# A perceiver block on one core: small sums leave TensorE for GpSimd, ScalarE and VectorE

## The reference

```python
def xattn(encoder_hc, decoder_hq, w_sim, b_sim, W_qv, b_qv):   # encoder_hc = layernorm(x), decoder_hq = ctx
    w1, w2, w3 = w_sim[:d], w_sim[d:2*d], w_sim[2*d:]
    Sim = (encoder_hc @ w1)[:, :, None] + (decoder_hq @ w2)[:, None, :] \
        + einsum('bid,bjd->bij', encoder_hc * w3, decoder_hq) + b_sim[0]
    A = softmax(Sim, axis=2)
    hq_hat = einsum('bij,bjd->bid', A, decoder_hq)
    Batt = softmax(max(Sim, axis=2), axis=1)
    hc_bar = einsum('bi,bid->bd', Batt, encoder_hc)[:, None, :]
    feats = concatenate([encoder_hc, hq_hat, encoder_hc * hq_hat, encoder_hc * hc_bar], axis=-1)
    return feats @ W_qv + b_qv
x = x + xattn(layernorm(x), ctx, ...)
x = x + linear_attention_with_rope(layernorm(x), ...)   # 16 heads
x = x + channel_mix(layernorm(x), ...)                  # token shift, relu squared, sigmoid gate
```

## Time and profile before

| | |
|---|---|
| median of 3 runs | 112.9 us (112.89 to 113.84) |
| the profiled execution's own time | 112.94 us |
| its span in the profile | 111.2 us |
| first pass, second pass, tail | to about 45 us, to about 91 us, to the end |

### The profile page before, as it was taken

The page is one execution under the profiler, slowest core; times in us unless marked ns, Lnnn a source line. Parts: engine busy times, 40 slices in busy tenths (PEclk is TensorE's granted clock), DMA queues, the critical chain, the costliest instruction groups (busy, mean ns, idle before and its releaser), DMA issues.

```text
span 111.2 us, 1842 instructions
## 1 busy us (share of the span) xinstructions
PE 105.4 (95%) x580; PEld 85.2 (77%) x581; DVE 93.6 (84%) x153; ACT 81.3 (73%) x170; POOL 26.2 (24%) x44
## 2 busy tenths in 40 slices
PE   5899999999999999999999999999999998998890
PEld 2368777676757668888989999898989997887680
DVE  1488999989999999989999999999999846684342
ACT  5076755889979986999999899989986625903450
POOL 2239100000023334124242423367230000100100
PEclk9999999999999999999999999999999999999999
DMA  3999999999999999999999999950000000000001
GB/s 79 382 410 422 420 416 423 420 420 420 410 422 417 420 413 420 422 404 398 439 401 410 422 422 420 414 201 3 3 0 0 0 6 0 0 0 3 6 0 47
DMA packets 8220, 29.82 MB, mean 268 GB/s; under 512 B 1042, under 2 KB 1298, under 8 KB 8082
## 3 DMA queue, kind: packets, MB, share of 16 engines
q1 hardware_dynamic: 8064, 29.69, 66.0%
q10 hardware_dynamic: 146, 0.01, 0.1%
HBM read 29.57 MB, written 0.13 MB: 267 GB/s over the span
## 4 chain that ended last, share of the span: by engine, by line
PE 91%; DVE 2%; DMA 2%; issue 1%; ACT 1%; POOL 1%; DVEq 0%; POOLq 0%; ACTq 0%
PE mixed_ps L988 18%; PE scores_ps L959 10%; PE mixed_ps L990 9%; PE scores_ps L916 9%; PE scores_ps L945 8%; PE scores_ps L931 8%; PE scores_ps L935 8%; PE scores_ps L970 3%; DMA x_sb<-x_dram 2%; PE scores_ps L1081 2%; PE mixed_ps L1133 2%; PE side_ps L1007 1%; PE scores_ps L1146 1%; PE side_ps L1124 1%; PE scores_ps L1007 1%
## 5 line engine op out<-in xcount | busy, mean ns | idle before, releaser
L689 DVE TENSOR_TENSOR pair<-raw,pair 128x1024 fp32r<-128x1024 f32 (+1 forms) x41 | 49.4, 1220 | 1.4 <-ACT pair L486 1.4
L486 ACT ACTIVATE pair<-raw 128x512 fp32r<-128x512 f32 (+1 forms) x41 | 33.3, 814 | 6.6 <-DMA raw<-keys_dram 5.1
L988 PE MATMUL mixed_ps<-pair,turned_high 128*128 128x512 f32 x84 | 32.3, 418 | 0.0
L990 PE MATMUL mixed_ps<-pair,turned_low 128*128 128x256 f32 x84 | 23.6, 281 | 0.0
L461 POOL CAST pair<-raw 128x512 fp32r<-128x512 f32 x22 | 13.6, 618 | 27.2 <-DVE pair L689 23.9
L988 PEld LDWEIGHTS mixed_ps<-pair,turned_high 128*128 128x128 f32 x84 | 15.8, 188 | 2.8
L712 DVE TENSOR_SCALAR_CACHE_REDUCE neg_scores<-scores_ps,neg_max 128x1024 f32<-128x1024 f32 (+2 forms) x14 | 16.0, 1145 | 0.4
L518 ACT ACTIVATE turned_high<-scores_ps 128x512 fp32r<-128x512 f32 (+1 forms) x23 | 13.4, 584 | 3.9 <-PE scores_ps L959 3.9
L990 PEld LDWEIGHTS mixed_ps<-pair,turned_low 128*128 128x128 f32 x84 | 16.0, 190 | 0.0
L719 DVE TENSOR_TENSOR turned_low<-scores_ps,turned_high 128x512 fp32r<-128x512 f32 (+1 forms) x23 | 15.3, 669 | 0.2 <-ACT turned_high L518 0.2
L959 PE MATMUL scores_ps<-ident,neg_scores 128*128 128x128 f32 x98 | 14.6, 272 | 0.0
(11 more groups left out here) (189 smaller groups left out, 129.6 us busy)
## 6 DMA issues: line engine op xcount, KB each, us to landing
raw<-keys_dram SPq DMA_DIRECT2D x24, 512.0 KB, 10.6
raw<-rows_dram SPq DMA_DIRECT2D x24, 512.0 KB, 8.7
w<-weights_dram SPq DMA_DIRECT2D x1, 1792.0 KB, 9.5
w<-weights_dram SPq DMA_DIRECT2D x2, 512.0 KB, 11.5
const<-const_dram SPq DMA_DIRECT2D x1, 832.0 KB, 10.9
raw<-keys_last_dram SPq DMA_DIRECT2D x1, 256.0 KB, 9.5
raw<-rows_last_dram SPq DMA_DIRECT2D x1, 256.0 KB, 6.1
x_sb<-x_dram SPq DMA_DIRECT2D x1, 128.0 KB, 2.3
```

The source lines that it names most:

```text
L486: nc.scalar.activation(pair[:, use % PAIR_BUFS, 0, 0:columns], raw[:, slot(item), 0:columns], ACT.Copy)\
L689: nc.vector.tensor_tensor(out=pair[:, use % PAIR_BUFS, 1, 0:columns], in0=raw[:, slot(item), 0:columns], in1=pair[:, use % PAIR_BUFS, 0, 0 ...
L988: nc.tensor.matmul(mixed_ps[:, :].rearrange("p (h d) -> p h d", h=2), probs_high, both[:, :, t * D:(t + 1) * D], start=(k == EARLY and t = ...
L990: last = nc.tensor.matmul(mixed_ps[:, 0:D], probs_low, rows_tile(high, t), start=False, stop=(k == LATE - 1 and end))
```

## The change

Three parts.

1. **hw1.** The three matmuls and the little load of b_sim go. A load of 128 equal rows of w1 and b_sim (128 x 257) is issued by SP behind keys 13. GpSimd multiplies `normed` by it ahead of its part of chunk 18, as soon as VectorE has chunk 15's low part; ScalarE sums the product behind chunk 19's high part; VectorE adds b_sim in the instruction that makes `sim_max`.
2. **Token attention.** ScalarE takes the exponential of all 128 spread columns in PSUM, with their sum. TensorE's three matmuls of round 8 go. In round 10 VectorE makes two fused products with a sum (`normed_t` half times the exponentials), between the reciprocal and the scaling; each waits for the one ahead.
3. **Centred input.** ScalarE makes it in the head, TensorE turns it (two transpositions ahead of those of `normed`), ScalarE copies it to SBUF after chunk 3. The matmuls of line 1065 go; VectorE adds it with the bias when it takes both halves of x1 out of PSUM. The square and the other copy of the first half are now made by ScalarE from VectorE's result.

```diff
@@ sync, keys loop
+                if k == 13:
+                    sp.dma_start(w1_rows[:, :], w1_rows_in).then_inc(w1_rows_loaded, 16)
@@ gpsimd
-            pool.wait_ge(b_c_done, DH)
-            nc.gpsimd.tensor_tensor(out=b_kept[:, :], in0=b_c[:, :, 0], in1=b_c[:, :, 1], op=ALU.add)\
-                .then_inc(b_kept_done, 1)
...
+                if k == 18:
+                    pool.wait_ge(low_done, split_before[15] + 1)
+                    pool.wait_ge(normed_done, DH)
+                    pool.wait_ge(w1_rows_loaded, 16)
+                    nc.gpsimd.tensor_tensor(out=hw1_parts, in0=normed[:, :], in1=w1_rows[:, 0:D], op=ALU.mult)\
+                        .then_inc(hw1_multiplied, 1)
@@ scalar
-            act.dma_start(bias[:, :], bias_in).then_inc(bias_loaded, 16)
...
+            center_x()
             act.wait_ge(q_done, DH)
...
-                if k == 8:
-                    center_x()
+                if k == 3:
+                    for a in range(DH):
+                        act.wait_ge(x_c_turned, a + 1)
+                        nc.scalar.activation(x_c_t[:, a, :], x_c_turn_ps[a], ACT.Copy).then_inc(x_c_t_done, 1)
+                if k == 19:
+                    act.wait_ge(hw1_multiplied, 1)
+                    nc.scalar.activation(hw1_parts, hw1_parts, ACT.Copy, accum_out=hw1_sum[:, :])\
+                        .then_inc(hw1_done, 1)
...
-                    nc.scalar.activation(batt[:, :], sim_max[:, :], ACT.Exp, bias=batt_neg_max[:, :])\
-                        .then_inc(batt_done, 1)
+                    nc.scalar.activation(batt_rows[:, :], batt_ps[:, 0:P], ACT.Exp, bias=batt_neg_max[:, :],
+                                         accum_out=batt_total[:, :]).then_inc(batt_done, 1)
...
+            act.wait_ge(x1_low_rows_done, 1)
+            nc.scalar.activation(x1_squared_t[:, 0, :], x1_t[:, 0, :], ACT.Square).then_inc(x1_low_squared, 1)
+            nc.scalar.activation(x1_kept_t[:, 0, :], x1_t[:, 0, :], ACT.Identity, bias=b_c[:, 0, 1:2])\
@@ vector
-                    dve.wait_ge(hc_bar_done, 1)
-                    nc.vector.reciprocal(batt_inv[:, :], batt_ps[:, DH:DH + 1]).then_inc(batt_inv_done, 1)
+                    dve.wait_ge(batt_done, 1)
+                    dve.wait_ge(normed_t_done, DH)
+                    nc.vector.reciprocal(batt_inv[:, :], batt_total[:, :]).then_inc(batt_inv_done, 1)
+                    for a in range(DH):
+                        if a > 0:
+                            dve.wait_ge(hc_bar_done, a)
+                        nc.vector.scalar_tensor_tensor(hc_parts[:, :], normed_t[:, a, :], 1.0, batt_rows[:, :],
+                                                       ALU.mult, ALU.mult, accum_out=hc_sum[:, a:a + 1])\
+                            .then_inc(hc_bar_done, 1)
+                    dve.wait_ge(hc_bar_done, DH)
...
+            for a, done in ((0, x1_low_rows_done), (1, x1_high_rows_done)):
+                dve.wait_ge(x1_projected, a + 1)
+                nc.vector.scalar_tensor_tensor(x1_t[:, a, :], x1_ps[a], b_c[:, a, 0:1], x_c_t[:, a, :],
+                                               ALU.add, ALU.add).then_inc(done, 1)
@@ tensor
+            pe.wait_ge(x_c_done, 1)
+            for a in range(DH):
+                nc.tensor.transpose(x_c_turn_ps[a], x_c[:, a * P:(a + 1) * P], ident[:, :]).then_inc(x_c_turned, 1)
             for a in range(DH):
                 pe.wait_ge(normed_done, a + 1)
...
-                    for a in range(DH):
-                        nc.tensor.matmul(hw1_ps, normed_t[:, a, :], vec[:, VC_W1 + a:VC_W1 + a + 1],
-                                         start=(a == 0), stop=False)
-                    nc.tensor.matmul(hw1_ps, ones[0:1, :], bias[0:1, 0:1],
-                                     start=False, stop=True).then_inc(hw1_done, 1)
...
-                    for a in range(DH):
-                        nc.tensor.matmul(batt_ps[:, a:a + 1], normed[:, a * P:(a + 1) * P], batt[:, :],
-                                         start=True, stop=True)
-                    nc.tensor.matmul(batt_ps[:, DH:DH + 1], ones[:, :], batt[:, :], start=True, stop=True)\
-                        .then_inc(hc_bar_done, 1)
...
-            pe.wait_ge(x_c_done, 1)
-            for o in range(DH):
-                nc.tensor.matmul(x1_ps[o], x_c[:, o * P:(o + 1) * P], ident[:, :], start=True, stop=False)
             pe.wait_ge(w_combined, DH)
-            features(0, 0, normed_t)
+            features(0, 0, normed_t, start=True)
```

More of the change, by code:

```diff
@@ L57, with build @@
 C_MASK, C_COS, C_SIN, C_BK, C_BV, C_COS_T, C_SIN_T, C_ALL = 0, *(P + D * n for n in range(7))
-def build(nc, x, keys_in, keys_last_in, rows_in, rows_last_in, weights_in, vec_in, bias_in, const_in, out):
+def build(nc, x, keys_in, keys_last_in, rows_in, rows_last_in, weights_in, vec_in, w1_rows_in, const_in, out):
     keys_full = keys_in.rearrange("(k p) n -> k p n", p=P)
@@ L120, in build @@
         vec = sb("vec", [P, VC])
-        bias = sb("bias", [1, 1])
         x_sb = sb("x_sb", [P, D])
@@ L126, in build @@
         neg_scores = sb("neg_scores", [P, S])
+        w1_rows = sb("w1_rows", [P, D + 1])
+        hw1_parts = neg_scores[:, S - D:S]
+        hw1_sum = sb("hw1_sum", [P, 1])
         turned_high = sb("turned_high", [P, TURNED_BUFS, CHUNK], F32R)
@@ L154, in build @@
         batt_neg_max = sb("batt_neg_max", [P, 1])
-        batt = sb("batt", [P, 1])
+        batt_rows = sb("batt_rows", [P, P])
+        batt_total = sb("batt_total", [P, 1])
+        hc_parts = sb("hc_parts", [P, P])
+        hc_sum = sb("hc_sum", [P, DH])
         batt_inv = sb("batt_inv", [P, 1])
         hc_bar = sb("hc_bar", [P, DH])
-        x_c = sb("x_c", [P, D])
+        x_c = neg_scores[:, S - 2 * D:S - D]
+        x_c_t = sb("x_c_t", [P, DH, P])
         x_neg_mean = sb("x_neg_mean", [P, 1])
@@ L169, in build @@
         b_c = sb("b_c", [P, DH, 2])
-        b_kept = sb("b_kept", [P, DH])
         mean_const = sb("mean_const", [P, 1])
@@ L211, in build @@
         batt_ps = banks[5]
-        hw1_ps = mixed_ps[:, 0:1]
         b_mean_ps = banks[4][:, 0:D]
+        x_c_turn_ps = (banks[5][:, 0:P], banks[5][:, P:2 * P])
         normed_turn_ps = (side_ps[:, 0:P], mixed_ps[:, 0:P])
@@ L235, in build @@
         vec_loaded = sem("vec_loaded")
-        bias_loaded = sem("bias_loaded")
+        w1_rows_loaded = sem("w1_rows_loaded")
         w_qv_loaded = [sem(f"w_qv_loaded{n}") for n in range(2)]
@@ L280, in build @@
         total_done = sem("total_done")
+        hw1_multiplied = sem("hw1_multiplied")
         hw1_done = sem("hw1_done")
@@ L292, in build @@
         b_c_done = sem("b_c_done")
-        b_kept_done = sem("b_kept_done")
         mean_const_done = sem("mean_const_done")
@@ L296, in build @@
         x_c_done = sem("x_c_done")
+        x_c_turned = sem("x_c_turned")
+        x_c_t_done = sem("x_c_t_done")
         w_combined = sem("w_combined")
@@ L544, in center_x @@
                 act.wait_ge(x_neg_mean_done, 1)
-                nc.scalar.activation(x_c[:, :], x_sb[:, :], ACT.Identity, bias=x_neg_mean[:, :]).then_inc(x_c_done, 1)
+                nc.scalar.activation(x_c, x_sb[:, :], ACT.Identity, bias=x_neg_mean[:, :]).then_inc(x_c_done, 1)
+            center_x()
             act.wait_ge(q_done, DH)
@@ L625, in _ @@
                                      scale=vec[:, VC_BQ + a:VC_BQ + a + 1]).then_inc(bq_cos_done, 1)
[L627 to L633 removed]
+            act.wait_ge(x1_low_rows_done, 1)
+            nc.scalar.activation(x1_squared_t[:, 0, :], x1_t[:, 0, :], ACT.Square).then_inc(x1_low_squared, 1)
+            nc.scalar.activation(x1_kept_t[:, 0, :], x1_t[:, 0, :], ACT.Identity, bias=b_c[:, 0, 1:2])\
                 .then_inc(x1_kept_done, 1)
             act.wait_ge(x1_high_rows_done, 1)
[L636 removed]
+            nc.scalar.activation(x1_kept_t[:, 1, :], x1_t[:, 1, :], ACT.Identity, bias=b_c[:, 1, 1:2])\
                 .then_inc(x1_kept_done, 1)
@@ L756, in _ @@
             dve.wait_ge(max_done, EVICTIONS + 1)
-            nc.vector.tensor_tensor(out=sim_max[:, :], in0=hw1_ps, in1=neg_max[:, EVICTIONS:EVICTIONS + 1],
-                                    op=ALU.subtract).then_inc(sim_max_done, 1)
+            nc.vector.scalar_tensor_tensor(sim_max[:, :], hw1_sum[:, :], w1_rows[:, D:D + 1],
+                                           neg_max[:, EVICTIONS:EVICTIONS + 1], ALU.add, ALU.subtract)\
+                .then_inc(sim_max_done, 1)
             rows_low(EARLY)
@@ L908, in scores @@
                     pe.wait_ge(b_mean_done, 1)
+                if k == 5:
+                    pe.wait_ge(x_c_t_done, DH)
                 if k >= 6:
@@ L1002, in open_sums, with features @@
                 nc.tensor.matmul(out_ps, idle[:, 0:P], idle[:, 0:D], start=True, stop=False)
-            def features(kind, a, source, stop=False):
+            def features(kind, a, source, start=False, stop=False):
                 for o in range(DH):
```

(4 more changed lines are left out.)

22 lines of the change are left out of this document (3 added, 19 removed).

## The result

| | before | after |
|---|---|---|
| median, same chip | 113.2 us (112.89 to 113.84) | 115.84 us (114.93 to 117.08) |
| the profiled execution's own time | 112.94 us | 114.93 us |
| its span | 111.2 us | 113.1 us |

The ratio of the runs is 1.0185 [1.0123, 1.0247]: the changed kernel is slower by 1.9%, or some 2.1 us. Forecast were 0.9. The two profiled executions differ by 1.99 us, and both have a mean granted clock of 1.00, so that they can be set side by side. Two of the four executions after (116.46 and 117.08) had a mean granted clock of 0.985; they lift the median, the ratio leaves the last out, and what that is comes at the end.

A forecast was written before the change was run, and what follows sets the result against it. VectorE's queue was taken to end the first pass, VectorE and TensorE both to fill the second; +0.13 + 0.85 - 0.05 = +0.93, taken as +0.9, on 112.94 gave 113.8 us, range 112.8 to 114.4.

The forecast's parts named there:

- The failed step: Part 3: dropping GpSimd's sum of two biases and the small DMA delays nobody, so no cost was counted.
- the cover named: First pass, GpSimd: the 256-column product, about 0.6 us, lies in 2.7 us of idle time and costs nothing.
- The place: First pass, keys 21: high part 0.8 us late against 0.70 reserve less 0.03 hand-over, so VectorE loses 0.13 us once.
- Its term: Second pass, part 2: VectorE's added 1.05 us less 0.20 reserve shifts the pass's end by +0.85 us.
- The insertion: Round 10 on VectorE: two fused products with sums add 1.05 us, bounds 0.42 and 1.3.
- The 0.48 for each product: Round 10 on VectorE: each fused product costs its duration of 0.35 us plus 0.13 for the wait.
- The hold by the cast: Round 10: GpSimd's cast holds VectorE's second product until about 0.48 us after the cast's start, adding 0.19 us.
- the reserve: End of second pass: VectorE's low probabilities can be 0.20 us late before TensorE waits.
- the cover named there: Head, part 3: two added transpositions, 0.3 us, fit TensorE's 1.00 us idle before 5.13; without it, up to 0.3.
- The first (hidden reserve of VectorE): Second pass: VectorE hides the products, TensorE stays the bound and gains 0.67 us; some 112.3 us, chance 0.1.
- the second: Rival on round 10: waits between VectorE instructions cost nothing, products 0.27 us each, insertion 0.44; 113.2 us, chance 0.12.
- The third: Rival: ScalarE's first-pass queue delays 1.2 us instead of 0.8, second pass starts 0.5 us later; 114.3 us, chance 0.18.

The follow-up runs named there:

- before_shifted: The kernel before with only the 4-byte `bias` tile's declaration moved behind `raw`, so `raw` starts at 48864; no instruction differs: 114.6 us, ratio 1.0097.
- after_padded: The changed kernel plus an unused 4-byte tile where `bias` was declared, so `raw` starts at 48896 again: 114.78 us, ratio 1.0129 to before.
- all_moved: Before plus part 3, token attention's products on GpSimd and sums on ScalarE, early copies each behind one rows high part, `raw` at 48896: 113.7 us, ratio 0.9998.
- reorder_centre: Before plus part 3, with ScalarE's early copies each directly behind one rows high part, `raw` at 48896: 113.2 us, ratio 0.9991.
- centre_alone: The kernel before with part 3 alone, but `bias` declared behind `raw`, which then starts at 48864: 114.5 us, ratio 1.0072.
- centre_aligned: The kernel before with part 3 alone and `bias` declared in its old place, `raw` at 48896: 113.23 us, ratio 1.0001.
- after_mended: The whole change with `raw` back at 48896 and ScalarE's early copies each directly behind one rows high part: 114.47 us, ratio 1.0069 to before.
- load_alone: The kernel before plus only the change's 131 KB load behind keys 13, which nothing uses, `raw` at 48896: 113.73 us, ratio 1.003.

## Why the prediction was wrong

**The failed step** is the last of part 3: "The dropped sum of two biases on GpSimd and the small DMA had nobody waiting." As an instruction that is so. But with the small DMA its tile went, too, and with that the address of the load buffers. I took the edits for what they do on engines and never asked what they move in memory. That is 1.0% (before_shifted), about 1.1 us; from after to after_padded it is 0.6%, with intervals that overlap, so that its size inside the whole change is known only roughly. With the address put back the kernel takes 1.3% [0.7, 1.9] more than before, and the forecast's 0.93 us, 0.8%, lies in that.

**The bound at the turn of the passes.** I saw that VectorE's queue "starts with a landing" in the first pass, but didn't follow the transfers to their end: ScalarE waits twice for rows, at 41.89 and 43.09, with early copies behind, and TensorE's first early product at 44.32 follows. There is hardly any cover: of the +1.37 at that product, +1.32 remain at the turn of chunk 8. That is where after paid for late landings, be it by the address or by the load, and not at keys 21.

**Part 1.** The 0.65 us of TensorE were taken up, as forecast. The load is worth 0.31 by the rate (131 KB), I had 0.4; the copy with a sum 0.40 as forecast; the product of GpSimd 0.74 instead of 0.6, under the cover named (its next instruction starts 1.59 us after it). The place was wrong: the high part of keys 21 is 0.23 late and not 0.8, because keys 18, for which ScalarE had waited 0.99 us, were there without a wait in this execution; its low part is at +0.02 where +0.13 stood. The load's 0.31 us shows at the landings of the rows instead, behind which there is no cover. In runs part 1 with the address kept is 1.0024 [0.998, 1.006], which doesn't tell 0.13 us from 0.3.

**Part 2.** Its term is right: +0.85 forecast at the end of the pass, 2.07 - 1.32 = +0.75 measured. The parts of it less so. The insertion was 0.84 to 0.86, forecast 1.05. The 0.48 for each product was 0.31: the wait costs 0.04 beyond the duration and not 0.13, and the duration is 0.27 rather than 0.35. The hold by the cast was 0.34 and not 0.19, only because the product came earlier into it: it was free about 0.49 us after the cast's start (64.67 + 0.49 = 64.82 + 0.34), for which I had worked out 0.48. Had it been held to the cast's end (65.29), as the Trainium skill's rule cited in the forecast has it (SBUF — State Buffer, Who interferes with whom), it would have lost 0.47: the measurement decides against the rule, here and at 54.57. That TensorE then goes by VectorE, waits 0.88 us, and gives its 0.67 back, came as argued. Of the reserve 0.14 was spent where I had 0.20: mix 23 moved by 2.07 and its low probabilities by 2.21.

**Part 3.** Costs nothing: 1.0001 [0.996, 1.004]. The head costs nothing in the end, but the cover named there isn't always present, the case that the forecast priced at up to 0.3. The query is at +0.37 in after and at -0.22 in after_padded, which has the same instructions. In after the four transpositions are 0.21 us apart, in after_padded 0.11 to 0.14; the first rows below are after's, the last two after_padded's:

```profile
5.41 0.42 PE L1048 MATMUL side_ps<-ident,normed 128*128 128x128 f32 x1
5.62 0.42 PE L1048 MATMUL mixed_ps<-ident,normed 128*128 128x128 f32 x1
4.97 0.27 PE L1049 MATMUL side_ps<-ident,normed 128*128 128x128 f32 x1
5.11 0.33 PE L1049 MATMUL mixed_ps<-ident,normed 128*128 128x128 f32 x1
```

The traces record full clock from 4.50 us on in after_padded, from 4.11 and 4.76 in all_moved and reorder_centre, where the query is early too; from 5.6 to 6.2 in centre_alone, centre_aligned and after_mended, where it is at +0.34 to +0.37 (after has no record of the rise). None of the ten traces without part 3 has it later than +0.04. So the two transpositions do delay the query where the clock rises late, and the first pass takes that up. The tail gains 0.1, forecast 0.05.

**The rivals.** The first (hidden reserve of VectorE) is excluded: the insertion came through. Of the second, the premise is half true, products 0.31 apart, but the hold ate what the cheap wait gave. The third named the right kind of loss, a start of the second pass that is too late, and 0.5 us for it; it put the cause in ScalarE's queue in the first pass, and measured are 1.3. With the measured terms: 1.37 at the first early product, less 0.05 to chunk 8, 0.75 to mix 23, less 0.10 in the tail, 1.97 in all; the two executions differ by 1.99.

**The base.** The profiled execution of before was "practically the median of 112.9" of three runs; over many more its median is 113.4 to 113.7. It began with quick transfers, and both reserves that I reckoned with, 0.70 us at keys 21 and 0.20 at the end of the second pass, were read from it alone. Beside after, on the same chip, its median was 113.2, so 0.3 us of the distance from 113.8 to 115.84 is the base.

## What to carry to other kernels

Read a diff for its declarations as for its instructions: a removed 4-byte tile moved the load buffers off a multiple of 256 and cost up to 1%, as much as any computation in it. Look up the start of each large load's buffer in the compiled program; declaring it first isn't enough, since here even the first tile starts at 16512, 128 past a multiple of 256. Follow each transfer to the queue that waits for it, and see what stands behind that wait in the same queue: there lateness is paid, and work that doesn't need the landing can stand in front of it. Moving work from one engine at 100% to another at 100% gained nothing: here 0.67 us left TensorE, 0.85 came to VectorE, and the pass ended 0.75 later. The same sums in GpSimd's and ScalarE's gaps cost nothing that could be measured, and gained nothing.

## What the runs showed of the hardware

- The start of a load's destination counts: in the three starts tried, 4096-byte packets take 159 ns in the median and 160.3 to 163.5 in the mean at a multiple of 256 in each partition (48896), 161 to 162 in the median and 164.6 to 165.4 in the mean at 224 past one (48864), and 161 and 164.8 at 64 past one (48960). The rate falls from 420 to about 410 GB/s.
- The second and third slice of the page, some 6 us of loads, ran at 311 to 414 GB/s in different executions with the same loads, worth about 1 us of landing time (the high part of chunk 9 1.12 us late in load_alone); what decides it was not tried.
- A fused product of VectorE with two inputs in SBUF, started 0.15 us behind a GpSimd cast, took 0.61 us instead of 0.27 in all five traces that have it: held until 0.48 to 0.49 us after the cast's start and not until its end at 0.62. A low part of 128x1024 started 0.36 us into a cast took 1.33 us, one started 0.56 us into it 1.22, its undisturbed time.
- In the tail the granted clock of TensorE fell to its lower level (1.2 GHz) for about 3.4 us in some executions of several kernels, shortly behind sixteen recorded products of one column; the same products stand in the trace of before at the same pace, and there it didn't fall. Rows of before_shifted by stretch (PE, PEld, DVE, ACT, POOL, clock, DMA share, GB/s):

```profile
100.00:104.00 4.00, 3.65 (x26) 3.15 (x25) 1.90 (x8) 1.16 (x3) 0.00 (x0) 1.00 0.01 2
104.00:108.00 4.00, 3.80 (x20) 3.02 (x21) 1.64 (x5) 1.86 (x6) 0.55 (x1) 0.59 0.02 4
```

It costs 1.05 to 1.1 us: before_shifted's shift goes from +1.11 at mix 23 to +2.18 at x3, and in reorder_centre, the same computation as centre_aligned, it is +0.18 at the third variance and +1.24 at x3. Two of the four executions of after had a mean granted clock of 0.985, as the profiled one of reorder_centre had; that fits the two longest (116.46 and 117.08), over 1 us above the others. What decides it stays open, and no edit was tried on it.
